# A network of eight blocks on one core: the routed feed-forward rewritten as one block, the grouped feed-forward with merged weights

## What is computed

```python
# layer 3 of 4 ("L2"): s = layer_norm(x + heads @ Wo) * gamma + beta      (causal attention)
def ffn(x, gamma, w1, b1, w2, b2):
    h = x / maximum(norm(x), 1e-12) * sqrt(128) * gamma
    return gelu(h @ w1 + b1) @ w2 + b2
s = einsum('bnd,d->bn', x, routing_token)            # 16 rows of 256 scores
for _ in range(50):                                  # one step depends on the last
    a = 0.1*log(8) - 0.1 * logsumexp((s + b) / 0.1)
    b = -relu(s + a)
scores = exp((s + a + b) / 0.1)
# the 128 best tokens of each row of 256 get the heavy branch as well:
out = ffn(x, light weights, hidden 64); out[best] += ffn(x[best], heavy weights, hidden 512)

# layer 4 of 4 ("L3"): eight groups of 512 tokens, each with its own weights, and no nonlinearity
h1 = einsum('gmh,goh->gmo', xg, W1) + b1             # 128 -> 512
h2 = einsum('gmo,gho->gmh', h1, W2) + b2             # 512 -> 128
```

## Time and profile before

| | |
|---|---|
| time, median of 3 runs | 5806.92 us (5806.7 to 5816.7) |
| the profiled execution's own time | 5807.41 us |
| its span, first to last instruction | 5805.6 us |
| mean granted TensorE clock | 0.92 of full speed |
| busy: PE, PEld | 4827.4 us (83%), 3362.5 us |
| busy: DVE, ACT, POOL | 3834.8 us (66%), 2866.4 us (49%), 2569.4 us (44%) |
| TensorE's busy tenths in 40 slices | `7699999999999999999999998533689996067874` |
| GpSimd's | `4476666766777677667766765012200000000000` |

### The profile page before, as it was taken

One profiled execution on the slowest core, in us unless ns is written; L12 is line 12 of the kernel. 1 busy time (PEld: TensorE's weight loads), 2 busy tenths in 40 slices (PEclk: granted clock), 3 DMA queues, 4 the chain that ended last, 5 costly groups with the idle time before them and its releaser, 6 DMA issues. The chain is left out here.

```text
span 5805.6 us, 144393 instructions
## 1 busy us (share of the span) xinstructions
PE 4827.4 (83%) x57263; PEld 3362.5 (58%) x57263; DVE 3834.8 (66%) x9149; ACT 2866.4 (49%) x6252; POOL 2569.4 (44%) x3065
## 2 busy tenths in 40 slices
PE   7699999999999999999999998533689996067874
PEld 3366666666666666666666666323556664045653
DVE  7677777777777777777777775666367777633421
ACT  2266665666666666666666655200256664322331
POOL 4476666766777677667766765012200000000000
PEclk9899999999999999999999999765889998587987
DMA  0211111111111111111111100011100000001001
GB/s 20 67 31 24 25 33 35 24 25 39 31 24 33 31 28 24 33 34 27 24 33 23 26 20 13 21 41 55 31 18 2 2 2 3 20 5 27 25 21 39
DMA packets 312161, 150.56 MB, mean 26 GB/s; under 512 B 146143, under 2 KB 301003, under 8 KB 311243
## 3 DMA queue, kind: packets, MB, share of 16 engines
q1 hardware_dynamic: 309451, 137.20, 9.8%
q0 software_dynamic: 2048, 4.20, 0.3%
HBM read 101.10 MB, written 27.41 MB: 22 GB/s over the span
## 5 line engine op out<-in xcount | busy, mean ns | idle before, releaser
L1435 POOL TENSOR_TENSOR loc_a<-loc_a,loc_b 128x512 f32<-128x512 f32 x768 | 976.7, 1274 | 231.6 <-DVE loc_b L1511 231.0
L1123 PE MATMUL psum<-loc_wqk,loc_xt 128*128 128x512 f32 x1536 | 828.0, 621 | 19.0 <-issue 8.3
L1186 PE MATMUL psum<-loc_m,xn_rows 128*128 128x128 f32 x6144 | 823.6, 277 | 3.9 <-DVE y_rows L1543 2.6
L1307 ACT ACTIVATE loc_sq<-psum 128x512 f32<-128x512 f32 x768 | 455.1, 593 | 680.6 <-PE psum L1123 680.0
L1460 POOL TENSOR_TENSOR loc_a<-loc_a,loc_rn 128x512 f32<-128x512 f32 x768 | 785.4, 1045 | 0.1
L1186 PEld LDWEIGHTS psum<-loc_m,xn_rows 128*128 128x128 f32 x6144 | 754.1, 193 | 45.6 <-issue 42.6
L1507 DVE TENSOR_TENSOR loc_a<-psum,loc_rope 128x512 f32<-128x512 f32 x768 | 523.4, 681 | 334.8 <-ACT loc_sq L1307 322.5
L1467 POOL TENSOR_TENSOR xn_cols<-xn_cols,loc_rec 128x512 f32<-128x512 f32 x384 | 394.5, 1048 | 687.2 <-DVE loc_rec L1538 687.1
L1344 ACT COPY xn_rows<-psum 128x512 f32<-128x512 f32 x768 | 411.7, 588 | 221.6 <-PE psum L1174 217.6
L1511 DVE TENSOR_TENSOR loc_b<-psum,loc_rope 128x512 f32<-128x512 f32 x768 | 520.7, 678 | 0.0
L1515 DVE TENSOR_REDUCE loc_n<-loc_sq 128x8 f32<-128x512 f32 x768 | 517.1, 673 | 0.0
(11 more groups left out here) (365 smaller groups left out, 8819.5 us busy)
## 6 DMA issues: line engine op xcount, KB each, us to landing
loc_x<-loc_shifted SPq DMA_DIRECT2D x192, 256.0 KB, 4.0
loc_shifted<-y_rows SPq DMA_DIRECT2D x144, 64.0 KB
loc_wqk<-in_L_ffn_Wqkv SPq DMA_DIRECT2D x24, 256.0 KB, 3.7
x_rows<-y_rows SPq DMA_DIRECT2D x96, 64.0 KB
x_rows<-y_rows SPq DMA_DIRECT2D x96, 63.5 KB
moe_w<-in_L_ffn_W SPq DMA_DIRECT2D x16, 256.0 KB, 4.6
l3a_qk<-l3a_rot SPq DMA_DIRECT2D x16, 256.0 KB, 2.1
grp_w<-in_L_ffn_W SPq DMA_DIRECT2D x16, 256.0 KB, 2.8
```

The lines of the kernel that those rows point to most:

```text
L1123: nc.tensor.matmul(ring("p", i, unit), xt[:, b % 2, t * P:(t + 1) * P], wqk[:, unit * 512:(unit + 1) * 512], start=True, stop=True).then_i ...
L1186: last = nc.tensor.matmul(y_bank[:, 0:P], u[:, i % 2, h // 2, h % 2, :], m[:, h, :], start=(h == 0), stop=(h == HEADS - 1))
L1307: nc.scalar.activation(sq[:, g % 2, :], ring("p", i, unit), ACT.Square).then_inc(sem["squared"], 1)
L1435: nc.gpsimd.tensor_tensor(part, part, b_[:, g % 2, :], ALU.add).then_inc(sem["added"], 1)
```

## The change

- **Attention of L2**: loads of gamma and beta and the call of `layer_norm_of_branch` are gone from its end.
- **Routed feed-forward**: one block, with no loop and no separate loads. SyncE issues all loads at its start. GpSimd squares all rows at the start. VectorE sums the squares in steps 10 and 13 of the 50, ScalarE takes a guess of the inverse root by logarithm and exponential behind step 16, GpSimd refines it once, scales the rows in eight groups, and scales the two first weights. TensorE turns the eight groups (four banks), ScalarE copies them into `xc` behind every second step from 34 on. Behind the steps VectorE computes the branch's statistics and root, evicts the outputs of group 0, makes the 32 comparisons in four rounds with one group's eviction behind each, normalises the branch's 32 tiles, and combines. GpSimd multiplies gamma and adds beta, four tiles at a time. `keep_outputs` adds the biases while evicting light and heavy outputs separately, so that TensorE's next light output waits for the eviction (`light_kept`) and no longer for the weighting.
- **Grouped feed-forward**: one block over all eight groups. Loads for all groups are issued at once, with a semaphore for each group. Only the second weight is turned; TensorE multiplies the two weights of a group into one of 128x128 (and the first bias through the second weight), and one product per tile of tokens follows.
- **Experts**: the semaphores of its indirect transfers are made once, at the program's start, and never cleared.

```diff
-names = ("sent", "turned", "cols_ready", "hid_done", "h_act", "h_dve", "out_done", "evicted", "added")
+names = ("turned", "cols_ready", "hid_done", "h_act", "h_dve", "out_done", "evicted", "added")
...
-taken_in, zero_taken_in = ctx.enter_context(signals(nc, [f"moe_taken{g}" for g in range(NT // 4)]))
...
-gamma, beta, xb = sb("gamma", [P, P]), sb("beta", [P, P]), sb("xb", [P, SEQ])
+xb = sb("xb", [P, SEQ])
...
-      (gamma[:, :], spread(dram["L2_attn_gamma"])), (beta[:, :], spread(dram["L2_attn_beta"]))])
+     [(att.wo[:, :, :], dram["L2_attn_Wo"].rearrange("(c p) n -> p c n", p=P)), (att.mask[:, :, :], att.mask_src)])
-layer_norm_of_branch(core, 1e-3, gamma[:, :], beta[:, :])
...
+(route_in, weights_in, norm_in), zero_in = ctx.enter_context(signals(nc, ["cd_route_in", "cd_weights_in", "cd_norm_in"]))
...
+sq = light
...
+    @block.sync
+    def _(sp):
+        sp.dma_start(rt[:, :], column(dram["L2_ffn_routing_token"])).then_inc(route_in, 16)
+        sp.dma_start(before[:, :, :], dram["before"]).then_inc(route_in, 16)
+        for dst, src in loads:
+            sp.dma_start(dst, src).then_inc(weights_in, 16)
+        sp.dma_start(gamma[:, :], spread(dram["L2_attn_gamma"])).then_inc(norm_in, 16)
+        sp.dma_start(beta[:, :], spread(dram["L2_attn_beta"])).then_inc(norm_in, 16)
...
+    @block.tensor
+    def _(pe):
+        def turn(g):
+            pe.wait_ge(sem["xr_ready"], g + 1)
...
+        def outputs(i):
+            pe.wait_ge(sem["light_gelu"], i + 1)
+            if i >= 1:
+                pe.wait_ge(sem["light_kept"], i)
...
+        for g in range(NGRP):
+            turn(g)
+        for i in range(NGRP + 1):
+            if i < NGRP:
+                hidden(i)
+            if i >= 1:
+                outputs(i - 1)
+    @block.scalar
+    def _(act):
+        def guess_root():
+            act.wait_ge(sem["n2_ready"], 2)
+            nc.scalar.activation(n2_log[:, :], n2[:, :], ACT.Ln).then_inc(sem["n2_log"], 1)
+            act.wait_ge(sem["n2_log"], 1)
+            nc.scalar.activation(guess[:, :], n2_log[:, :], ACT.Exp, scale=-0.5).then_inc(sem["rn_guess"], 1)
+        def copy_columns(g):
+            act.wait_ge(sem["turned"], g + 1)
+            nc.scalar.copy(xc[:, g * 512:(g + 1) * 512], turn_bank(g)[:, :]).then_inc(sem["cols_ready"], 1)
+        nc.scalar.preload_act_table_set("natural_log_exp_and_others")
+        for k in range(ROUTE_ITERS):
+            act.wait_ge(sem["top_ready"], k + 1)
+            act.wait_ge(sem["capped"], k + 1)
+            nc.scalar.activation(e[:, :], u[:, :], ACT.Exp, bias=top[:, 0:1], accum_out=total[:, :]).then_inc(sem["sum_ready"], 1)
+            act.wait_ge(sem["sum_ready"], k + 1)
+            nc.scalar.activation(log[:, :], total[:, :], ACT.Ln).then_inc(sem["log_ready"], 1)
+            if k == 16:
+                guess_root()
+            if k >= 34 and k % 2 == 0:
+                copy_columns(k // 2 - 17)
+        act.wait_ge(sem["z_ready"], 1)
+        nc.scalar.activation(e[:, :], u[:, :], ACT.Exp).then_inc(sem["score_ready"], 1)
...
+    @block.gpsimd
+    def _(pool):
+        after = chain(pool, sem["pool_step"])
+        for half in range(2):
+            x = core.xn[:, half * HALF:(half + 1) * HALF, :]
+            nc.gpsimd.tensor_tensor(sq[:, half * HALF:(half + 1) * HALF, :], x, x, ALU.mult).then_inc(sem["squared"], 1)
+        pool.wait_ge(sem["rn_guess"], 1)
+        after(nc.gpsimd.tensor_tensor(step[:, :], guess[:, :], guess[:, :], ALU.mult))
+        after(nc.gpsimd.tensor_tensor(step[:, :], step[:, :], n2[:, :], ALU.mult))
+        after(nc.gpsimd.tensor_scalar(step[:, :], step[:, :], -0.5 * float(np.sqrt(P)), 1.5 * float(np.sqrt(P)), ALU.mult, ALU.add))
+        nc.gpsimd.tensor_tensor(rn[:, :], guess[:, :], step[:, :], ALU.mult).then_inc(sem["rn_ready"], 1)
+        pool.wait_ge(sem["rn_ready"], 1)
+        for g in range(NGRP):
+            tiles = slice(G * g, G * (g + 1))
+            nc.gpsimd.tensor_tensor(core.y[:, tiles, :], core.xn[:, tiles, :],
+                                    rn[:, tiles].rearrange("p (t a) -> p t a", a=1).to_broadcast([P, G, P]), ALU.mult).then_inc(sem["xr_ready"], 1)
+        pool.wait_ge(weights_in, 16 * len(loads))
+        nc.gpsimd.tensor_scalar(w1l[:, :], w1l[:, :], gl[:, 0:1], None, ALU.mult).then_inc(sem["weights_scaled"], 1)
+        nc.gpsimd.tensor_scalar(w1h[:, :], w1h[:, :], gh[:, 0:1], None, ALU.mult).then_inc(sem["weights_scaled"], 1)
+        pool.wait_ge(norm_in, 32)
+        for g in range(NGRP):
+            rows = core.s[:, G * g:G * (g + 1), :]
+            pool.wait_ge(sem["rows_normed"], G * (g + 1))
+            nc.gpsimd.tensor_tensor(rows, rows, wide(gamma[:, :], G), ALU.mult).then_inc(sem["gained"], 1)
+            pool.wait_ge(sem["gained"], g + 1)
+            nc.gpsimd.tensor_tensor(rows, rows, wide(beta[:, :], G), ALU.add).then_inc(sem["norm_stored"], 1)
     @block.vector
...
+            after(nc.vector.tensor_reduce(n2[:, rows], sq[:, rows, :], AX.X, ALU.add))
+            nc.vector.tensor_scalar(n2[:, rows], n2[:, rows], 1e-24, None, ALU.max).then_inc(sem["n2_ready"], 1)
...
+        def combine(i):
+            dve.wait_ge(sem["light_kept"], i + 1)
+            dve.wait_ge(sem["heavy_kept"], i + 1)
+            for j in range(G * i, G * (i + 1)):
+                last = nc.vector.scalar_tensor_tensor(out=core.y[:, j, :], in0=core.y[:, j, :], scalar=weight[:, j:j + 1],
+                                                      in1=light[:, j, :], op0=ALU.mult, op1=ALU.add)
+            last.then_inc(sem["combined"], 1)
...
+            if k in (10, 13):
+                measure(k // 12)
...
+        for j in range(NT):
+            last = nc.vector.bn_stats(stats[:, j, :], core.s[:, j, :])
+        after(last)
+        for j in range(NT):
+            last = nc.vector.bn_aggr(mv[:, j, :], stats[:, j, :])
+        after(last)
+        after(nc.vector.tensor_scalar(mv[:, :, 1], mv[:, :, 1], 1e-3, None, ALU.add))
+        rsqrt(nc, after, rstd[:, :], mv[:, :, 1], tmp[:, :])
+        keep_outputs(0)
+        dve.wait_ge(sem["spread_"], 32)
+        for i in range(1, 5):
+            for j in range(8 * (i - 1), 8 * i):
+                rank(j)
+            keep_outputs(i)
...
+        for j in range(NT):
+            nc.vector.tensor_scalar(core.s[:, j, :], core.s[:, j, :], mv[:, j, 0:1], rstd[:, j:j + 1], ALU.subtract,
+                                    ALU.mult).then_inc(sem["rows_normed"], 1)
+            if j == 15:
+                keep_outputs(5)
+        keep_outputs(6)
+        for i in range(NGRP - 1):
+            combine(i)
+        keep_outputs(NGRP - 1)
+        combine(NGRP - 1)
...
+loaded, zero_loaded = ctx.enter_context(signals(nc, [f"grp_loaded{g}" for g in range(NG)]))
...
+with nc.Block() as block:
+    @block.sync
+    def _(sp):
+        for g in range(NG):
+            sp.dma_start(w2[:, g, :, :], dram["L3_ffn_W2"][g, :, :].rearrange("p (c o) -> p c o", o=P)).then_inc(loaded[g], 16)
+            sp.dma_start(w1[:, g, :, :], dram["L3_ffn_W1"][g, :, :].rearrange("(c p) h -> p c h", p=P)).then_inc(loaded[g], 16)
+            sp.dma_start(b1[:, g, :], dram["L3_ffn_b1"][g, :].rearrange("(c p) -> p c", p=P)).then_inc(loaded[g], 16)
+            sp.dma_start(b2[:, g, :], dram["L3_ffn_b2"][g:g + 1, :].to_broadcast([P, P])).then_inc(loaded[g], 16)
+    @block.tensor
+    def _(pe):
+        def turn(g):
+            pe.wait_ge(loaded[g], 64)
+            if g >= 2:
+                pe.wait_ge(sem["w_ready"], g - 1)
+            for c in range(CH):
+                last = nc.tensor.transpose(turn_bank[g % 2][:, c * P:(c + 1) * P], w2[:, g, c, :], core.ident[:, :])
+            last.then_inc(sem["turned"], 1)
+        def merge(g):
+            pe.wait_ge(sem["w_ready"], g + 1)
+            if g >= 2:
+                pe.wait_ge(sem["merged_ready"], 2 * (g - 1))
+            for c in range(CH):
+                nc.tensor.matmul(merge_bank[g % 2][:, 0:P], w1[:, g, c, :], w2t[:, g % 2, c, :], start=(c == 0), stop=(c == CH - 1),
+                                 skip_group_check=True)
+            for c in range(CH):
+                last = nc.tensor.matmul(merge_bank[g % 2][:, P:2 * P], b1[:, g, c:c + 1].to_broadcast([P, P]), w2t[:, g % 2, c, :],
+                                        start=(c == 0), stop=(c == CH - 1), skip_group_check=True)
+            last.then_inc(sem["merged"], 1)
+        def outputs(g):
+            pe.wait_ge(sem["merged_ready"], 2 * (g + 1))
+            if g >= 2:
+                pe.wait_ge(sem["stored"], g - 1)
+            for t in range(TILES):
+                at = g * GTOK + t * P
+                last = nc.tensor.matmul(out_bank[g % 2][:, t * P:(t + 1) * P], core.xnt[:, at:at + P], merged[:, g % 2, :], start=True, stop=True)
             last.then_inc(sem["out_done"], 1)
 
+        for n in range(NG + 2):
+            if n < NG:
+                turn(n)
+            if 0 <= n - 1 < NG:
+                merge(n - 1)
```

(42 more changed lines are left out.)

368 lines of the change are left out of this document (126 added, 242 removed).

## The result

The changed kernel takes 5585.87 us (median; 5578.07 to 5592.48) against 5811.81 (5806.7 to 5817.54) for the kernel before beside it: ratio 0.961, 95% interval 0.9597 to 0.9623. The forecast was 5606 in a range of 5583 to 5630, a ratio of 0.965. The time lies inside the range, near its low end: the change gained 226 us where the sum said 201. The profiled execution took 5578.07 us, span 5576.2.

A forecast was written before the change was run, and what follows sets the result against it. Two rewritten stages were seen as strings of blocks with one engine working while others stand. Gains of 92.3 (routed), 107.5 (grouped), 0.5 and 0.9 sum to 201.2 us, giving 5606; own range 5594 to 5620, widened to 5583 to 5630.

The forecast's parts named there:

- T0: End of the 50 routing steps in the routed stage; forecast at 4988.5, from 5005.25 in the kernel before.
- held normalisations: Routed stage behind T0: each GpSimd instruction holds one VectorE row normalisation, four tiles taking 3.0 us, not 1.0.
- exposed reductions: Routing steps: two VectorE reductions of the squares lengthen their steps by 2.2 us each, 4.4 in all.
- rivals B: Grouped stage stays at the low clock because short bursts wait on evictions: 23 us more, 5629; chance 0.10.
- C: Loads set the grouped stage's pace, each group costing 5.06 us: +8 us, 5614; chance 0.07.
- D: Routing steps: copies wholly exposed (+4.3) and nothing let through beside GpSimd (+3.5): 5614; chance 0.06.
- E: Slower than before: small-head attention between the two stages left at the low clock, 5843 at 0.50; chance 0.01.
- rival A: Routed stage: GpSimd does not hold small instructions; copies -5.5 us, steps -7.5, giving 5593; chance 0.15.
- step 1: Start of the routed block: copies into rtm, held by GpSimd's squares, end at about 4892.6, not 4921.69; gain 29.1 us.
- step 2: Work put into the 50 routing steps: +12.3 us in sum, 7.5 of it from GpSimd holding VectorE.
- two or three steps near the 18th last about 5: Sign expected in the routing steps beside GpSimd's instructions: two or three steps of about 5 us.
- step 4: Grouped stage: 3.8 us a group, last write about 41 us after first load; gain 107.5 us.

The follow-up runs named there:

- Experiments 1: Changed kernel with both reductions of the squares and the root guess ahead of the step loop: copies to T0 85.5 us, 91.6 in the changed kernel.
- 2: Changed kernel with GpSimd's gamma and beta only after all 32 normalisations: routed stage ends at T0 + 94.0, T0 + 89.9 in the changed kernel.
- 3: Changed kernel with GpSimd multiplying and adding tile by tile, not four tiles at a time: routed stage ends at T0 + 88.1 against T0 + 89.9.
- 5: Changed kernel with all 32 comparisons ahead of the evictions of groups 1 to 4: routed stage ends at T0 + 112.4 against T0 + 89.9.
- 6: Kernel before with only the changed kernel's grouped stage: 0.9812 of the kernel before; first load to last write 35.29 us.
- 7: Also called unmerged: changed kernel's one-block grouped stage, but both weights turned, none merged: stage 75.05 us against 35.2; whole execution 5658.26 us.
- norm_on_act: Changed kernel with the 32 normalisations on ScalarE and the first groups' combinations moved up: routed stage ends at T0 + 81.75 against T0 + 89.9.
- biases_behind: Changed kernel with each group's bias loads behind the next group's weights, on their own semaphore: first transpose at 4.34 us, grouped stage end at 33.89 against 35.2.

## Why the prediction was right, and where it was off

**Right, by its own steps.** The mechanisms held: a VectorE-paced stage behind T0 with TensorE just covered (rounds 9.61 for 9.8, T0 + 53.9 for T0 + 54.1 at the end of the last eviction), held normalisations (22.9 for 23.4), exposed reductions (2.0 each for 2.2), hidden guess and copies, no wait on `light_kept` in the comparison rounds and one of 6.9 us for the seventh light eviction, one clock rise in the grouped stage. Of rivals B, C, D and E none came: the grouped stage at a mean clock of 0.84 with groups at 3.12, the copies hidden, and the stretch between the two stages, the small-head attention in it, at a clock of 0.84 (0.83 before). Experiments 1, 2, 3 and 5 show the hold and the interleaving as causes, and 6 and 7 the one block and the merging. The forecast's own range was 5594 to 5620, though, and 5586 lies below it: the time is inside the stated range only because that was widened to 5583 for rival A, which came in part (5.5 us of the copies and at most 4.3 of the steps, out of 13). Every step's miss but one, the slower first load, went the same way, toward less time.

**Off: step 1, the copies into `rtm`.** The failed step is "the 16 copies into rtm are of the held kind". They are copies, but of one column, and such ones pass. That is 5.5 of the 6.3 us; the other 0.8 are a landing 0.4 sooner and copies 0.4 shorter than taken. The squares, mis-sized as well (4.6 for 3.6), cost nothing, since nothing waited for their end.

**Off: step 2, the hold in the steps.** "If each GpSimd instruction lets one through" was right for three of the five instructions; the term was 7.5 and measured 4.1. It also let all 14 GpSimd instructions hold, and the eight scalings of the rows did nearly all of it. Its own sum was off by half a microsecond: 14 instructions at five to a step of 1.42 are 4.0 us of progress, not 3.5. The sign "two or three steps near the 18th last about 5" came as two steps of 3.1. Rival A (0.15) said that small instructions pass at all. Its first half came, its second by half: what counts is one column against many, and one SBUF operand against two.

**Off: step 4, the group.** 3.12 for 3.8, eight times, is 5.4 us; another 1.7 lie in low-clock start and drain, and 1.4 went to the slower first load. The products' own rate was nearly in the earlier trace rows: 16 in 3.81 us at a granted clock of 1.00, of which about 0.17 is the end of the last product (an estimate from the rows above, 1.06 long and 0.89 apart), so 0.228 each and not 0.24. The gaps of 0.35 were an allowance for waits that the pipelining over three groups removes.

**Not of the change.** 9.0 us lie in stretches whose arithmetic is the same, the largest of them 2.7 in the attention ahead of the routed stage and 4.1 between the routed and the grouped one. In two profiles of the changed kernel the first combination starts at 3656.35 and at 3681.72, so such differences need no cause in the change (the mark is ScalarE's table load at that combination's start). By medians the change gains 226 us in one measurement and 223 in the other; the terms above make 201 + 19 = 220. What the last 3 to 6 us are stays open.

## What to carry over

Ask of every VectorE instruction beside a busy GpSimd how many SBUF operands it reads and how many columns. In these runs four kinds passed: copies and scalings of one column, reductions, accumulating comparisons with one operand, and reads from PSUM. Scalings and copies of 16 columns and more, and instructions with two SBUF operands, even of one column, waited for the end of GpSimd's instruction, one let through by each. So small GpSimd instructions cost their neighbours less than large ones. A stage of many equal groups gains most from being one block with its loads issued ahead (74 of 114 us here), more than from saving half its products (40). Work put beside other work should go first where its engine already waits (10 us for the scores here), and only then into the slack of a loop. An effect of 1 or 2 us in a stage has to be set against how much that stage differs between traces of the same code (1.9 us for the grouped one).

## What the runs showed of the hardware that I had not expected

- One-column copies and scalings of VectorE pass beside GpSimd (143 to 154 ns, 189 to 196 ns over 50 steps), a scaling of 16 columns does not (0.17 to 0.45 us), and a one-column instruction with two SBUF operands doesn't either (140 to 984 ns).
- An accumulating comparison of 256 columns with one SBUF operand isn't held (469 to 481 ns beside 21.7 us of GpSimd work), its sister with two is (483 to 1381).
- GpSimd multiplies 2048 columns by themselves in 3.6 us, 1.75 ns a column; 512 columns of the branch by gamma take 1.27, 2.5 ns a column.
- One wait of 1.62 us was followed by about 3 us at the low clock (norm_on_act: 0.50 from 5041.0 to 5043.5), after 38.6 us at 1.00 in which TensorE was busy all the time.
- The same kernel's untouched first part differed by 25 us between two profiled executions, while ratios to the kernel before agreed within 0.0001 (0.9610 and 0.9611). On one chip it differed by 21 us between two programs with the same first part (its end at 3659.99 in biases_behind and at 3680.94 in unmerged).
